# Transformer layers with routed experts: the order of queries and keys, scores and transposes of two pairs of heads, and the bank that the second pair's queries and keys are written to

## Chip, cores and metric

One core of one Trainium2 chip runs the whole kernel. The metric is the device time of one execution in microseconds. "us" below is microseconds. The core's engines are TensorE (PE in the rows; PEld is its weight load), VectorE (DVE), ScalarE (ACT), GpSimd (POOL) and SyncE (SP). Each engine takes its own instructions strictly in the order in which the program issues them, and waits on semaphores where another engine's result is needed; so a wait holds up everything issued behind it on that engine.

## What is computed

The input is 8 sequences of 256 tokens with 128 features. There are two stages, each an attention and then a feed-forward layer with 8 routed experts:

```python
x = x + attention_a(layernorm(x))   # 16 heads of 64, learned relative bias, softmax
x = x + experts(layernorm(x))       # one of 8 experts for each token, relu, gate
x = x + attention_b(layernorm(x))   # causal in blocks, keys and values from a 128-wide latent
x = x + experts(layernorm(x))
```

In the attention, for each head: `scores = q @ k.T * scale + bias` (or a causal mask), `softmax`, `@ v`, and then the output projection over all heads. All matrices are float32; the products with weights are made from three passes of high and low parts (`three`), and the high parts are made by ScalarE and the low ones by VectorE.

## The kernel before

The unit of the attention is a pair of heads of one sequence: a stage has NB = 8 sequences with 8 pairs each, NU = 64 units. Every engine runs a function `step(s)` for s = 0, 1, 2, ..., and in each step works on several units at once, so that the units overlap as in a pipeline. U0 and B0 are the number of units and sequences before the stage. The order within a step is written out by hand for each engine. Here an even step and the odd step behind it are called a round; e is the even unit and o the odd unit of a round.

For unit u the work goes like this:
- TensorE, `QK(u)`: queries and keys, six matmuls, into one bank of PSUM, `PT_` = ps[0]. Before it writes, it waits until the unit before has been copied out (`a_t`).
- ScalarE, `T(u)` (line 825): copies the bank to `a_qk[u % 2]`.
- TensorE, `S(u)` (line 528): the scores of the two heads, eight matmuls on 64 rows each, into a bank for each head: ps[1] and ps[2] for an even unit, ps[3] and ps[7] for an odd one. The two heads lie in the two halves of the array.
- VectorE, `S(u)` (line 1148): adds bias or mask, takes the row minimum of the negated scores and frees the banks (`v_mn`).
- ScalarE, `expo(u)` (line 857): exponentials and row sums, two steps later. VectorE, `weigh` (line 1159): reciprocals. GpSimd, `weigh` (line 315): normalises.
- TensorE, `TR(u)` (line 419), four steps later: eight transposes (six in the causal stage) into ps[4] and ps[5]; ScalarE copies the first head's (line 844), VectorE the second's (line 1177).
- TensorE, `PV(u)` (line 565): eight matmuls with weights of 64 columns. ScalarE and VectorE take the result apart in `keep` (lines 779 and 1028).

Around that, once for each sequence of 8 units: `values` (four times, 512 columns), the layer norm's transposes (`pre_b`), the latent (`pre_c`, stage 1 only), the output projection `out` (24 matmuls), its transposes back `out_2`, the second norm (`sums`, `post_a`, `post_b`), the router's logits (`post_c`), counts (`post_d`) and places (`choose`, `place` on VectorE, for some sequences).

TensorE's order in a round is, before the change: QK(e), values, pre_b, counts or logits, TR(e-4), out | QK(o), pre_c, out_2, post_b, TR(o-4), S(e), S(o), PV(e-4), PV(o-4). The bar divides the even from the odd step. VectorE's: keep, pre_b, post_a, TR(e-4), choose or place | pre_c, out_2, TR(o-4), reciprocals of e-2, `sums`, `pre_a2`, S(e), S(o), reciprocals of o-2, `pre_a`. VectorE's part of the logits (line 1215), `choose` and `place` are in `routes`, the last call of a step.

Small results of TensorE go to banks that `spare` hands out: `turn` is the list of banks of the step, in the order in which they are taken, and `claim` makes TensorE wait until the bank's last reader is done (`held`). The scores claim their banks in the same way.

Of the kernel before, what the change touches and what calls it, by code (L numbers as in the profile page):

```python
# [47 lines left out]
QUARTERS = (0, 2, 1, 3)  # L48
VALUES = [{2: [(0, 0)], 3: [(0, 2)], 4: [(0, 1), (0, 3)]}, {0: [(0, 0)], 1: [(0, 2)], 2: [(0, 1)], 4: [(0, 3)]}]
for _v in VALUES:  # L50
    _v |= {8 * b + 2 * i - 2: [(b, n)] for b in range(1, NB) for i, n in enumerate(QUARTERS)}
VALUE_NO = {(b, n): 4 * b + i for b in range(NB) for i, n in enumerate(QUARTERS)}
# [60 lines left out]
def build(nc, t):  # L113
# [291 lines left out]
    def spare(use, done, n, bank=None):  # L405

        if bank is None:
            bank = turn.pop(0)
            turn.append(bank)
        bank_of[use] = bank  # L410
        return claim(bank, done, n)
# [31 lines left out]
    def pe_steps(st):  # L443
# [29 lines left out]
        def values(b, n):  # L473
            k = 4 * B0 + VALUE_NO[(b, n)] + 1
            j, half_ = n // 2, n % 2
            if st == 0 and b == 0 and k <= 2:
                bank_of[("v", st, b, n)] = 3 + k
                PX = PP[k - 1]
            else:
                PX = spare(("v", st, b, n), a_vs, k)  # L480
            key_ready(b)
            if b == 0:
                pe.wait_ge(a_wv, 3 if st else 2)
                pe.wait_ge(v_wv, 3 if st else 2)
            r = slice(512 * half_, 512 * half_ + 512)
            c = slice(128 * j, 128 * j + 128)
            three(PX[:, :], kH[b % 2][:, c], kL[b % 2][:, c], wvh[:, r], wvl[:, r]).then_inc(t_v, 1)

        def QK(u):

            b, c = divmod(u, 8)
            if c == 0:
                pe.wait_ge(a_x, B0 + b + 1)
                pe.wait_ge(v_x, B0 + b + 1)
                key_ready(b)
            if st == 0 and u in (0, 4):
                pe.wait_ge(a_m, 2 + u // 2)
                pe.wait_ge(v_m, 2 + u // 2)
            if U0 + u:
                pe.wait_ge(a_t, U0 + u)  # L500
            r, r2_ = slice(128 * c, 128 * c + 128), slice(1024 + 128 * c, 1024 + 128 * c + 128)
            if U0 + u != NU:
                three(PT_[:, 0:256], wqkh[:, r], wqkl[:, r], a_xth[b % 2][:, :], a_xtl[b % 2][:, :])
            three(PT_[:, 256:512], wqkh[:, r2_], wqkl[:, r2_], kH[b % 2][:, :], kL[b % 2][:, :]).then_inc(t_t, 1)

# [196 lines left out]
        def step(s):  # L702
            n = s - F0
            turn[:] = (7, 3) if s < 0 or s >= NU else (3, 7, 1, 2) if s % 2 else (1, 2, 3, 7)
            if 0 <= s < NU:
                QK(s)
            if st == 0 and s == 0:
                value_weights()
# [4 lines left out]
            if st and (b := pre_at(s, "c", st)) is not None:  # L713
                pre_c(b)
                if b == 0:
                    first_queries()
            if (b := at(s, 13)) is not None and b < NB - 1:
                out_2(b)
            if s < NU:
# [68 lines left out]
    def act_steps(st):  # L788
# [10 lines left out]
        def pre_b(b):  # L799
            act.wait_ge(t_x, B0 + b + 1)  # L800
            inputs_free(b)
            if st and b >= 2:
                act.wait_ge(t_lat, b - 1)
            act_high(a_xth[b % 2][:, :], ps[bank_of[("x", B0 + b)]][:, 0:256], a_x)

        def pre_c(b):
            act.wait_ge(t_lat, b + 1)
            inputs_free(b)
            act_high(a_lth[b % 2][:, :], ps[bank_of[("l", b)]][:, 0:256], a_l)

# [10 lines left out]
        def T(u):  # L821
            act.wait_ge(t_t, U0 + u + 1)
            if U0 + u >= 2:
                act.wait_ge(t_s, U0 + u - 1)
            act.copy(a_qk[(U0 + u) % 2][:, :], PT_[:, :]).then_inc(a_t, 1)  # L825

        def values(b, n):
            j, half_ = n // 2, n % 2
            r = slice(512 * half_, 512 * half_ + 512)
            act.wait_ge(t_v, 4 * B0 + VALUE_NO[(b, n)] + 1)  # L830
            if B0 + b >= 2:
                act.wait_ge(t_pv, U0 + 8 * (b - 2) + 8)
            act.copy(a_v[b % 2][:, j, r], ps[bank_of[("v", st, b, n)]][:, :]).then_inc(a_vs, 1)

# [11 lines left out]

        def expo(u, heads=(0, 1)):
            U = U0 + u
            ring, mn, sm = a_ring[U % 4], a_mn[U % 4], a_sm[U % 4]
            for hh in heads:  # L850
                act.wait_ge(v_mn, 2 * (U0 + u) + hh + 1)
                if U >= 4 and hh == 0:
                    act.wait_ge(v_rs, U0 + u - 3)
                for it in range(2):
# [3 lines left out]
                                       bias=mn[:, q], scale=-1.0, accum_out=sm[:, q])  # L858
            if 1 in heads:
                i.then_inc(a_ex, 1)  # L860

        def out(b):
            act.wait_ge(t_out, 7 * st + b + 1)
            if 7 * st + b:
                act.wait_ge(t_o2, 7 * st + b)
            act.copy(a_oT[:, :], ps[bank_of[("o", B0 + b)]][:, 0:256]).then_inc(a_oTs, 1)

        def post_b(b):
            act.wait_ge(t_pp, B0 + b + 1)
            if B0 + b:  # L870
                act.wait_ge(t_lg, B0 + b)
            act.copy(a_pT[:, :], ps[bank_of[("p", B0 + b)]][:, 0:256]).then_inc(a_pTs, 1)

        def post_d(b):
# [3 lines left out]
            if r:  # L878
                act.wait_ge(v_used, r)
            act.copy(cnt[:, 0:2 * n8], ps[bank_of[("cnt", r)]][:, 0:2 * n8]).then_inc(a_cnt, 1)  # L880

        def extra(s):
            for g in range(2 if s == 4 else 0):
                act.wait_ge(t_wo, g + 1)
                act_high(wo[:, 4 * g:4 * g + 4, 0:128],
                         ps[bank_of[("wo", g)]][:, :].rearrange("p (c n) -> p c n", c=4), a_wo)

# [5 lines left out]
        def XT(g):  # L893
            n = 128 * (GROUPS[g][1] - GROUPS[g][0])
            act.wait_ge(t_fx, NG * st + g + 1)
            if NG * st + g >= 2:
                act.wait_ge(t_fh, NF * (st - (g < 2)) + GROUPS[g - 2][1])
            act.copy(f_xt[g % 2][:, 0:n], ps[bank_of[("xt", st, g)]][:, 0:n]).then_inc(a_fx, 1)

# [45 lines left out]
        def step(s):  # L945
# [19 lines left out]
            if not (s % 2 and 3 <= s < NU):  # L965
                if st and (b := pre_at(s, "c", st)) is not None:
                    pre_c(b)
                if s < NU:
                    after(s)
# [124 lines left out]
    def dve_steps(st):  # L1094
# [18 lines left out]
        def pre_b(b):  # L1113
            low(a_xtl[b % 2][:, :], ps[bank_of[("x", B0 + b)]][:, 0:256], a_xth[b % 2][:, :], a_x, B0 + b + 1, v_x)

        def pre_c(b):
            low(a_ltl[b % 2][:, :], ps[bank_of[("l", b)]][:, 0:256], a_lth[b % 2][:, :], a_l, b + 1, v_l)

# [72 lines left out]
        def out_2(b):  # L1191
            xx = x[:, 2 * b:2 * b + 2, :]
            dve.wait_ge(t_o2, 7 * st + b + 1)
            dve.tensor_tensor(xx, ps[bank_of[("o2", B0 + b)]][:, 0:256].rearrange("p (a d) -> p a d", a=2), xx,
                              ALU.add).then_inc(v_res, 1)
# [15 lines left out]
        def post_c(b):  # L1211
            dve.wait_ge(t_lg, B0 + b + 1)
            if st == 0 and b == 0:
                dve.wait_ge(d_ln, 48)
            dve.tensor_tensor(
                lg[:, 2 * b:2 * b + 2, :],
                ps[bank_of[("lg", B0 + b)]][:, 0:16].rearrange("p (t e) -> p t e", t=2),
                brb[:, :].rearrange("p (t e) -> p t e", t=1).broadcast_to((128, 2, NE)), ALU.add).then_inc(v_lg, 1)
# [122 lines left out]
        def step(s):  # L1341
# [203 lines left out]
```

## Time and profile before

| | us |
|---|---|
| median of 3 runs | 686.56 |
| lowest and highest | 685.88, 688.58 |
| the profiled execution, whole | 687.1 |
| its span on the core | 685.9 |
| TensorE busy in it | 652.9 |
| ScalarE busy in it | 533.3 |
| VectorE busy in it | 482.1 |
| GpSimd busy in it | 358.8 |

Stage 0's attention lies from about 13 to 295 us, its experts to about 370 us; stage 1's attention goes from there to about 615 us, its experts to the end. The starts of matmuls are recorded and their ends are modelled, so matmuls overlap in the record; where TensorE's own rate matters, the distance between starts is what to read.

### The profile page before, as it was taken

To read this page: it belongs to the slowest core of one execution; us is meant where nothing else is said; L and a number is where in the kernel's file an instruction comes from. 1 tells how busy PE (TensorE), PEld (TensorE's weight loads), DVE (VectorE), ACT (ScalarE), POOL (GpSimd) and SP (SyncE) were. 2 spreads that over 40 slices of the span, in tenths; PEclk is the share of its full clock that TensorE was granted. 3 is DMA by queue.
4 is the path that set the end of the run, shared out by engine and by line. 5 is a ranking of instruction groups with operands and counts; after the bars stand their busy time and mean duration, and the time that the engine had idled before them with its cause. 6 is when DMAs were issued, how large, how long until landed. Compare 5 with 4: busy or idle time off the path is not lost.

```text
span 685.9 us, 17753 instructions
## 1 busy us (share of the span) xinstructions
PE 652.9 (95%) x5406; PEld 549.8 (80%) x5406; DVE 482.1 (70%) x2145; ACT 533.3 (78%) x1774; POOL 358.8 (52%) x672
## 2 busy tenths in 40 slices
PE   6899999999999999989898999999999999989897
PEld 5678787888888888778796788878888888868886
DVE  4876767776786767877564676687868776896644
ACT  3888888787887978765573998898989898885464
POOL 3444545465556554635452555464755575553645
PEclk9999999999999999999998999999999999999999
DMA  9999999997000000134411000000000000031130
GB/s 266 303 304 304 231 284 308 300 293 216 1 2 17 17 1 5 37 87 161 126 43 55 2 2 1 1 3 9 17 11 1 10 24 3 17 87 44 58 106 13
DMA packets 67468, 64.65 MB, mean 94 GB/s; under 512 B 7793, under 2 KB 63998, under 8 KB 67120
## 3 DMA queue, kind: packets, MB, share of 16 engines
q1 hardware_dynamic: 62624, 56.41, 29.7%
q0 software_dynamic: 3136, 6.34, 2.7%
q10 hardware_dynamic: 1616, 0.79, 0.5%
q8 instruction: 45, 0.74, 0.5%
q14 instruction: 47, 0.39, 0.2%
HBM read 19.93 MB, written 44.75 MB: 94 GB/s over the span
## 4 chain that ended last, share of the span: by engine, by line
PE 82%; DVE 9%; issue 3%; ACT 2%; POOL 1%; DMA 1%; another core or an unknown queue 1%; SPq 0%; DVEq 0%; POOLq 0%; ACTq 0%
PE ps L419 16%; PE ps L565 14%; PE ps L528 14%; PE ps L414 10%; PE ps L416 8%; PE ps L415 8%; PE ps L668 5%; PE ps L682 4%; DVE ring L1148 2%; DMA wvn<-in_w_qkv 1%; PE ps L602 1%; PE ps L620 1%; ACT f_ht L906 1%; DVE f_ys L1314 1%
## 5 line engine op out<-in xcount | busy, mean ns | idle before, releaser
L315 POOL TENSOR_SCALAR ring<-ring,rs 128x256 f32<-128x256 f32 (+1 forms) x500 | 218.1, 453 | 221.2 <-DVE rs L1159 220.8
L857 ACT ACTIVATE ring<-ring,mn 128x256 f32<-128x256 f32 (+1 forms) x512 | 243.5, 489 | 0.0
L419 PE MATMUL ps<-ident,ring 128*128 128x128 f32 x896 | 120.4, 274 | 2.5 <-POOL ring L315 2.4
L528 PE MATMUL ps<-qk 64*128 64x256 f32 (+1 forms) x1024 | 115.0, 363 | 0.2 <-ACT qk L825 0.2
L565 PE MATMUL ps<-pt,v 128*64 128x256 f32 (+1 forms) x1024 | 111.9, 359 | 1.9 <-DVE pt L1175 1.3
L419 PEld LDWEIGHTS ps<-ident,ring 128*128 128x128 f32 x896 | 102.4, 142 | 8.2 <-POOL ring L315 3.5
L857 ACT ACTIVATION_READ_ACCUMULATOR ring<-ring,mn 128x1 f32 x512 | 104.5, 204 | 0.0
L565 PEld LDWEIGHTS ps<-pt,v 128*64 128x64 f32 x1024 | 65.8, 136 | 46.1 <-issue 14.5
L528 PEld LDWEIGHTS ps<-qk 64*128 64x128 f32 x1024 | 82.5, 187 | 18.0 <-issue 9.3
L825 ACT COPY qk<-ps 128x512 f32<-128x512 f32 x128 | 74.8, 585 | 24.9 <-PE ps L416 23.3
L1148 DVE CUSTOM_DVE_ANT_0 ring<-ps,cm 128x128 f32<-128x128 f32 (+1 forms) x256 | 73.5, 350 | 6.0 <-PE ps L528 6.0
L1177 DVE COPY pt<-ps 128x512 f32<-128x512 f32 x64 | 44.1, 689 | 35.1 <-PE ps L419 35.1
L906 ACT ACTIVATE f_ht<-ps,f_w 128x128 f32<-128x128 f32 x136 | 38.1, 373 | 35.2 <-PE ps L668 33.6
L414 PE MATMUL ps<-xth,wqkh 128*128 128x256 f32 x192 | 65.2, 340 | 0.0
L682 PE MATMUL ps<-w,f_ht 128*128 (+1 forms) x400 | 53.2, 278 | 4.1 <-ACT f_ht L906 2.4
L1148 DVE CUSTOM_DVE_ANT_0 ring<-ps,T 128x256 f32<-128x256 f32 x136 | 55.5, 417 | 0.0
L416 PE MATMUL ps<-xtl,wqkh 128*128 128x256 f32 x192 | 54.4, 283 | 0.0
L415 PE MATMUL ps<-xth,wqkl 128*128 128x256 f32 x192 | 54.1, 282 | 0.0
L779 ACT ACTIVATE oh<-ps 128x512 fp32r<-128x512 f32 x64 | 38.3, 599 | 20.0 <-PE ps L565 20.0
L682 PEld LDWEIGHTS ps<-w,f_ht 128*128 128x128 f32 x400 | 48.3, 192 | 6.2 <-issue 6.0
L414 PEld LDWEIGHTS ps<-xth,wqkh 128*128 128x128 f32 x192 | 36.4, 190 | 18.6 <-issue 17.4
L1148 DVE CUSTOM_DVE_ANT_1 ring<-ps,T 128x256 f32<-128x256 f32 x120 | 50.0, 417 | 0.0
(209 smaller groups left out, 1350.3 us busy)
## 6 DMA issues: line engine op xcount, KB each, us to landing
xs_scratch<-padt SPq DMA_DIRECT2D x16, 2064.0 KB, 21.6
f_xs<-xs_scratch SPq DMA_DIRECT2D x50, 129.0 KB, 2.4
w<-in_W SPq DMA_DIRECT2D x16, 256.0 KB, 6.2
xs_scratch<-padt SPq DMA_DIRECT2D x2, 1677.0 KB, 20.3
T<-in_bias SPq DMA_DIRECT2D x2, 512.0 KB, 8.2
T<-in_bias SPq DMA_DIRECT2D x1, 1024.0 KB, 10.8
bu<-in_w_kv_up SPq DMA_DIRECT2D x1, 1024.0 KB, 8.2
row<-in_x SPq DMA_DIRECT2D x1, 768.0 KB, 12.8
```

The costliest lines, as they stand in the source:

```text
L315: i = pool.tensor_scalar(ring[:, hh, it, 0:w], ring[:, hh, it, 0:w], rs[:, q], 1.0, ALU.mult, ALU.mult)
L414: pe.matmul(out, ah, bh, start=first, stop=False)
L415: pe.matmul(out, al, bh, start=False, stop=False)
L416: return pe.matmul(out, ah, bl, start=False, stop=last)
L419: return pe.transpose(out, src, ident[:, :])
L528: i = pe.matmul(PS[u % 2][hh][:, 256 * it:256 * it + w], qk[rows, 128 * it:128 * it + 128], qk[rows, 256:256 + w], start=True, stop=True)
L565: i = pe.matmul(PO[64 * hh:64 * hh + 64, col + lo:col + 256], a_v[b % 2][:, jt, 128 * c + 64 * hh:128 * c + 64 * hh + 64], a_pt[(U0 + u) % ...
L682: i = pe.matmul(y_bank(n)[:, 0:128], f_ht[n % 3][:, 128 * f:128 * f + 128], w2[:, bass.ds(e * 4 + f, 1), :].rearrange("p a n -> p (a n)"), ...
L825: act.copy(a_qk[(U0 + u) % 2][:, :], PT_[:, :]).then_inc(a_t, 1)
L857: i = act.activation(ring[:, hh, it, 0:w], ring[:, hh, it, 0:w], ACT.Exp, bias=mn[:, q], scale=-1.0, accum_out=sm[:, q])
L906: i = act.activation(f_ht[n % 3][:, r], h_bank(n)[:, r], ACT.Relu, bias=first_layer(n)[:, 640 + f:641 + f])
L1148: i = dve.tensor_tensor_reduce(ring[:, hh, it, 0:w], bank[:, 256 * it:256 * it + w], table(st, 2 * c + hh, it), 1.0, BIG, ALU.add, ALU.min ...
```

## The change

1. TensorE: `QK(e)` and `QK(o)` come together in the even step. `QK(o)` writes to ps[7], the bank of the second head's scores of the odd unit, and so waits until VectorE has read the scores of unit o-2 from it; `QK(e)` keeps ps[0]. ScalarE copies both together.
2. TensorE: `S(e)` comes first in the odd step, ahead of TR(o-4); `S(o)` comes behind TR(o-4) as before. VectorE takes S(e) first in the odd step too, and S(o) where both were.
3. The spare banks of a step: (3, 1, 2) in even steps, (0, 1) in odd ones, where they were (1, 2, 3, 7) and (3, 7, 1, 2).
4. `out_2` moves behind `S(o)` on TensorE, and behind TR(o-4) on VectorE.
5. Values that lay in odd steps move to even ones (one in either stage).
6. ScalarE: the exponentials of a unit are made in one go behind TR, where the even unit's second head came in the odd step; `post` and `pre` work lies at one place.

TensorE's order in a round after it: QK(e), QK(o), values, pre_b, counts or logits, TR(e-4), out | S(e), pre_c, post_b, TR(o-4), S(o), out_2, PV(e-4), PV(o-4).

```diff
+    PQ = (ps[0], ps[7])
...
         def QK(u):
 
+            claim(7 * (u % 2), a_t, U0 + u + 1)
             b, c = divmod(u, 8)
...
-            if U0 + u:
-                pe.wait_ge(a_t, U0 + u)
...
-                three(PT_[:, 0:256], wqkh[:, r], wqkl[:, r], a_xth[b % 2][:, :], a_xtl[b % 2][:, :])
+                three(PQ[u % 2][:, 0:256], wqkh[:, r], wqkl[:, r], a_xth[b % 2][:, :], a_xtl[b % 2][:, :])
...
-            turn[:] = (7, 3) if s < 0 or s >= NU else (3, 7, 1, 2) if s % 2 else (1, 2, 3, 7)
-            if 0 <= s < NU:
+            turn[:] = (7, 3) if s < 0 or s >= NU else (0, 1) if s % 2 else (3, 1, 2)
+            if s % 2 == 0 and 0 <= s < NU:
                 QK(s)
+                QK(s + 1)
+            if s % 2 and 1 <= s < NU:
+                S(s - 1)
...
-            if (b := at(s, 13)) is not None and b < NB - 1:
-                out_2(b)
             if s < NU:
                 after(s)
             if 4 <= s < NU + 4:
...
             if (b := at(s, 12)) is not None and b < NB - 1:
                 out(b)
             if s % 2 and 1 <= s < NU:
-                S(s - 1)
                 S(s)
+            if (b := at(s, 13)) is not None and b < NB - 1:
+                out_2(b)
...
# ScalarE
-            if 0 <= s < NU:
+            if s % 2 == 0 and 0 <= s < NU:
                 T(s)
+                T(s + 1)
...
-            if s % 2 and 3 <= s < NU:
-                if st and (b := pre_at(s, "c", st)) is not None:
-                    pre_c(b)
-                after(s)
-                expo(s - 3, (1,))
...
             if 2 <= s <= NU:
-                expo(s - 2, (0, 1) if s % 2 or s == NU else (0,))
+                expo(s - 2)
...
# VectorE
+            if s % 2 and 1 <= s < NU:
+                S(s - 1)
             if (b := pre_at(s, "b", st)) is not None:
                 pre_b(b)
...
-            if (b := at(s, 13)) is not None and b < NB - 1:
-                out_2(b)
...
             if 4 <= s < NU + 4:
                 TR(s - 4)
+            if (b := at(s, 13)) is not None and b < NB - 1:
+                out_2(b)
...
             if s % 2 and 1 <= s < NU:
-                S(s - 1)
                 S(s)
```

## Rows read from the trace of the kernel before

**Rows 1.** The page, busy time, and its 40 slices for TensorE and its clock.

```profile
PE 652.9 (95%) x5406; PEld 549.8 (80%) x5406; DVE 482.1 (70%) x2145; ACT 533.3 (78%) x1774; POOL 358.8 (52%) x672
...
PE   6899999999999999989898999999999999989897
...
PEclk9999999999999999999998999999999999999999
```

**Rows 2.** Busy time by stretches, columns named in the first line.

```profile
core 0: us, PE busy (x) PEld busy (x) DVE busy (x) ACT busy (x) POOL busy (x), PEclk, DMA share, GB/s
...
100.00:150.00 50.00, 50.00 (x406) 40.45 (x405) 38.69 (x173) 42.13 (x132) 28.56 (x54) 1.00 1.10 304
...
450.00:500.00 50.00, 49.86 (x445) 41.40 (x445) 38.16 (x198) 45.57 (x169) 31.08 (x65) 1.00 0.04 12
```

**Rows 3.** TensorE's waits, whole span: total us, times, longest.

```profile
PE ps L414 <- DVE mn L1148: 2.8, 2, 2.3
...
PE ps L528 <- ACT qk L825: 0.2, 1, 0.2
```

**Rows 4.** Timeline, TensorE, one round of stage 0: start, us, line, work, count.

```profile
124.75 0.28 PE L416 MATMUL ps<-xtl,wqkh 128*128 128x256 f32 x1
124.87 1.03 PE L419 MATMUL ps<-ident,ring 128*128 128x128 f32 x8
125.83 2.00 PE L528 MATMUL ps<-qk 64*128 64x256 f32 x16
127.76 1.95 PE L565 MATMUL ps<-pt,v 128*64 128x256 f32 x16
129.64 0.39 PE L414 MATMUL ps<-xth,wqkh 128*128 128x256 f32 x1
129.86 0.27 PE L415 MATMUL ps<-xth,wqkl 128*128 128x256 f32 x1
129.97 0.28 PE L416 MATMUL ps<-xtl,wqkh 128*128 128x256 f32 x1
```

**Rows 5.** Timeline, TensorE, the same round, short windows that cut groups apart.

```profile
125.63 0.27 PE L419 MATMUL ps<-ident,ring 128*128 128x128 f32 x1
...
126.15 0.38 PE L528 MATMUL ps<-qk 64*128 64x256 f32 x2
...
127.45 0.38 PE L528 MATMUL ps<-qk 64*128 64x256 f32 x2
...
128.03 0.39 PE L565 MATMUL ps<-pt,v 128*64 128x256 f32 x2
...
129.32 0.39 PE L565 MATMUL ps<-pt,v 128*64 128x256 f32 x2
```

**Rows 6.** Timeline, a round with logits: the even unit's transposes and VectorE behind.

```profile
150.83 1.07 PE L419 MATMUL ps<-ident,ring 128*128 128x128 f32 x8
...
151.94 0.69 DVE L1177 COPY pt<-ps 128x512 f32<-128x512 f32 x1 [1.54 <-PE ps L419]
...
152.55 0.17 DVE L1215 TENSOR_TENSOR lg<-ps,brb 128x16 f32<-128x16 f32 x1
```

**Rows 7.** Timeline, a round with `out` and `sums`, stage 0.

```profile
135.01 0.29 PE L416 MATMUL ps<-ol,wo 128*128 128x256 f32 x1
...
135.33 0.37 ACT L866 COPY oT<-ps 128x256 f32<-128x256 f32 x1 [1.64 <-PE ps L416]
...
136.30 0.42 DVE L1194 TENSOR_TENSOR row<-ps,row 128x256 f32<-128x256 f32 x1 [3.01 <-PE ps L419]
...
137.87 0.26 DVE L1033 BATCH_NORM_STATS2 s<-row 128x6 f32<-128x128 f32 x1
...
138.99 0.41 DVE L1148 CUSTOM_DVE_ANT_1 ring<-ps,T 128x256 f32<-128x256 f32 x1
```

**Rows 8.** Timeline, VectorE, a round with `place`.

```profile
124.96 0.16 DVE L1066 COPY bas<-run 128x8 f32<-128x8 f32 x1
...
126.95 0.17 DVE L1081 CAST posi<-posf 128x4 int32<-128x4 f32 x1
127.03 0.69 DVE L1177 COPY pt<-ps 128x512 f32<-128x512 f32 x1
```

**Rows 9.** Timeline, a round of stage 1.

```profile
445.67 1.60 PE L528 MATMUL ps<-qk 64*128 64x128 f32 x16
...
447.20 1.52 PE L565 MATMUL ps<-pt,v 128*64 128x256 f32 x16
...
447.73 0.28 DVE L1148 CUSTOM_DVE_ANT_0 ring<-ps,cm 128x128 f32<-128x128 f32 x1
...
448.65 0.39 PE L414 MATMUL ps<-xth,wqkh 128*128 128x256 f32 x1
```

More of the change, by code:

```diff
@@ L48 @@
 QUARTERS = (0, 2, 1, 3)
-VALUES = [{2: [(0, 0)], 3: [(0, 2)], 4: [(0, 1), (0, 3)]}, {0: [(0, 0)], 1: [(0, 2)], 2: [(0, 1)], 4: [(0, 3)]}]
+VALUES = [{2: [(0, 0)], 3: [(0, 2)], 4: [(0, 1)], 6: [(0, 3)]}, {0: [(0, 0)], 2: [(0, 2)], 4: [(0, 1), (0, 3)]}]
 for _v in VALUES:
-    _v |= {8 * b + 2 * i - 2: [(b, n)] for b in range(1, NB) for i, n in enumerate(QUARTERS)}
+    for _s, _q in ((8 * b + 2 * i - 2, (b, n)) for b in range(1, NB) for i, n in enumerate(QUARTERS)):
+        _v.setdefault(_s, []).append(_q)
 VALUE_NO = {(b, n): 4 * b + i for b in range(NB) for i, n in enumerate(QUARTERS)}
@@ L409, in spare @@
             turn.append(bank)
-        bank_of[use] = bank
+        bank_of[use] = ps[bank]
         return claim(bank, done, n)
@@ L476, in values @@
             if st == 0 and b == 0 and k <= 2:
-                bank_of[("v", st, b, n)] = 3 + k
-                PX = PP[k - 1]
+                PX = bank_of[("v", st, b, n)] = PP[k - 1]
             else:
@@ L498, in QK @@
                 pe.wait_ge(v_m, 2 + u // 2)
-            if U0 + u:
-                pe.wait_ge(a_t, U0 + u)
             r, r2_ = slice(128 * c, 128 * c + 128), slice(1024 + 128 * c, 1024 + 128 * c + 128)
             if U0 + u != NU:
-                three(PT_[:, 0:256], wqkh[:, r], wqkl[:, r], a_xth[b % 2][:, :], a_xtl[b % 2][:, :])
-            three(PT_[:, 256:512], wqkh[:, r2_], wqkl[:, r2_], kH[b % 2][:, :], kL[b % 2][:, :]).then_inc(t_t, 1)
+                three(PQ[u % 2][:, 0:256], wqkh[:, r], wqkl[:, r], a_xth[b % 2][:, :], a_xtl[b % 2][:, :])
+            three(PQ[u % 2][:, 256:512], wqkh[:, r2_], wqkl[:, r2_], kH[b % 2][:, :], kL[b % 2][:, :]).then_inc(t_t, 1)
         def first_queries():
@@ L803, in pre_b @@
                 act.wait_ge(t_lat, b - 1)
-            act_high(a_xth[b % 2][:, :], ps[bank_of[("x", B0 + b)]][:, 0:256], a_x)
+            act_high(a_xth[b % 2][:, :], bank_of[("x", B0 + b)][:, 0:256], a_x)
         def pre_c(b):
@@ L808, in pre_c @@
             inputs_free(b)
-            act_high(a_lth[b % 2][:, :], ps[bank_of[("l", b)]][:, 0:256], a_l)
+            act_high(a_lth[b % 2][:, :], bank_of[("l", b)][:, 0:256], a_l)
         def keep(u):
@@ L824, in T @@
                 act.wait_ge(t_s, U0 + u - 1)
-            act.copy(a_qk[(U0 + u) % 2][:, :], PT_[:, :]).then_inc(a_t, 1)
+            act.copy(a_qk[(U0 + u) % 2][:, :], PQ[u % 2][:, :]).then_inc(a_t, 1)
         def values(b, n):
@@ L832, in values @@
                 act.wait_ge(t_pv, U0 + 8 * (b - 2) + 8)
-            act.copy(a_v[b % 2][:, j, r], ps[bank_of[("v", st, b, n)]][:, :]).then_inc(a_vs, 1)
+            act.copy(a_v[b % 2][:, j, r], bank_of[("v", st, b, n)][:, :]).then_inc(a_vs, 1)
         def TR(u):
@@ L845, in TR, with expo @@
             i.then_inc(a_pt0, 1)
-        def expo(u, heads=(0, 1)):
+        def expo(u):
             U = U0 + u
             ring, mn, sm = a_ring[U % 4], a_mn[U % 4], a_sm[U % 4]
-            for hh in heads:
+            for hh in range(2):
                 act.wait_ge(v_mn, 2 * (U0 + u) + hh + 1)
@@ L858, in expo @@
                                        bias=mn[:, q], scale=-1.0, accum_out=sm[:, q])
-            if 1 in heads:
-                i.then_inc(a_ex, 1)
+            i.then_inc(a_ex, 1)
         def out(b):
@@ L865, in out @@
                 act.wait_ge(t_o2, 7 * st + b)
-            act.copy(a_oT[:, :], ps[bank_of[("o", B0 + b)]][:, 0:256]).then_inc(a_oTs, 1)
+            act.copy(a_oT[:, :], bank_of[("o", B0 + b)][:, 0:256]).then_inc(a_oTs, 1)
         def post_b(b):
@@ L871, in post_b @@
                 act.wait_ge(t_lg, B0 + b)
-            act.copy(a_pT[:, :], ps[bank_of[("p", B0 + b)]][:, 0:256]).then_inc(a_pTs, 1)
+            act.copy(a_pT[:, :], bank_of[("p", B0 + b)][:, 0:256]).then_inc(a_pTs, 1)
         def post_d(b):
@@ L879, in post_d @@
                 act.wait_ge(v_used, r)
-            act.copy(cnt[:, 0:2 * n8], ps[bank_of[("cnt", r)]][:, 0:2 * n8]).then_inc(a_cnt, 1)
+            act.copy(cnt[:, 0:2 * n8], bank_of[("cnt", r)][:, 0:2 * n8]).then_inc(a_cnt, 1)
         def extra(s):
@@ L885, in extra @@
                 act_high(wo[:, 4 * g:4 * g + 4, 0:128],
-                         ps[bank_of[("wo", g)]][:, :].rearrange("p (c n) -> p c n", c=4), a_wo)
+                         bank_of[("wo", g)][:, :].rearrange("p (c n) -> p c n", c=4), a_wo)
         def products(*ns):
@@ L897, in XT @@
                 act.wait_ge(t_fh, NF * (st - (g < 2)) + GROUPS[g - 2][1])
-            act.copy(f_xt[g % 2][:, 0:n], ps[bank_of[("xt", st, g)]][:, 0:n]).then_inc(a_fx, 1)
+            act.copy(f_xt[g % 2][:, 0:n], bank_of[("xt", st, g)][:, 0:n]).then_inc(a_fx, 1)
         def relu(n):
@@ L964, in step @@
                 pre_b(b)
[L965 to L969, printed above, removed]
+            if st and (b := pre_at(s, "c", st)) is not None:
+                pre_c(b)
+            if s < NU:
+                after(s)
             if 4 <= s < NU + 4:
@@ L1113, in pre_b @@
         def pre_b(b):
-            low(a_xtl[b % 2][:, :], ps[bank_of[("x", B0 + b)]][:, 0:256], a_xth[b % 2][:, :], a_x, B0 + b + 1, v_x)
+            low(a_xtl[b % 2][:, :], bank_of[("x", B0 + b)][:, 0:256], a_xth[b % 2][:, :], a_x, B0 + b + 1, v_x)
         def pre_c(b):
-            low(a_ltl[b % 2][:, :], ps[bank_of[("l", b)]][:, 0:256], a_lth[b % 2][:, :], a_l, b + 1, v_l)
+            low(a_ltl[b % 2][:, :], bank_of[("l", b)][:, 0:256], a_lth[b % 2][:, :], a_l, b + 1, v_l)
         def keep(u):
@@ L1193, in out_2 @@
             dve.wait_ge(t_o2, 7 * st + b + 1)
-            dve.tensor_tensor(xx, ps[bank_of[("o2", B0 + b)]][:, 0:256].rearrange("p (a d) -> p a d", a=2), xx,
+            dve.tensor_tensor(xx, bank_of[("o2", B0 + b)][:, 0:256].rearrange("p (a d) -> p a d", a=2), xx,
                               ALU.add).then_inc(v_res, 1)
@@ L1216, in post_c @@
                 lg[:, 2 * b:2 * b + 2, :],
-                ps[bank_of[("lg", B0 + b)]][:, 0:16].rearrange("p (t e) -> p t e", t=2),
+                bank_of[("lg", B0 + b)][:, 0:16].rearrange("p (t e) -> p t e", t=2),
                 brb[:, :].rearrange("p (t e) -> p t e", t=1).broadcast_to((128, 2, NE)), ALU.add).then_inc(v_lg, 1)
@@ L1224, in extra @@
             for g in range(2 if s == 4 else 0):
-                low(wo[:, 4 * g:4 * g + 4, 128:256], ps[bank_of[("wo", g)]][:, :].rearrange("p (c n) -> p c n", c=4),
+                low(wo[:, 4 * g:4 * g + 4, 128:256], bank_of[("wo", g)][:, :].rearrange("p (c n) -> p c n", c=4),
                     wo[:, 4 * g:4 * g + 4, 0:128], a_wo, g + 1, v_wo)
```

## Prediction

> **What bounds the kernel now.** First the page's busy times and slices: TensorE is busy 652.9 of 685.9 us, and its clock was granted in full nearly everywhere [rows 1]. Then the stretches, since a mean over the span says nothing of a stage: in the attention of stage 0 TensorE is busy 50.00 of 50 us, in that of stage 1 49.86; ScalarE has 42.13 and 45.57 there, VectorE 38.69 and 38.16 [rows 2]. Then its waits: for the copy of queries and keys, which a second bank is to hide, it waited 0.2 us in the whole span, and for a bank of scores 2.8 us, of which 2.3 at once at the start [rows 3]. So in both attentions the time is what TensorE needs to issue its matmuls one behind the other, and no other engine holds it up. What the change can win by waits is about 3 us; what it adds to TensorE's own order counts in full.
>
> That order has a price that busy time hides, since the ends of matmuls are modelled. It is in the distances of starts [rows 4, 5]. A transpose follows a QK matmul after 0.12 us (124.75 to 124.87), which is a QK matmul's own distance (129.86 to 129.97): going between these two costs nothing. Eight transposes would take 0.87 us at 0.11 each (124.87 to 125.63 is seven), but the scores start 0.20 behind the last transpose (125.63 to 125.83), 0.09 too late. The second couple of score matmuls comes 0.32 behind the first (125.83 to 126.15), where the block has 0.21 as a rule (16 matmuls, 8 couples, from 125.83 to 127.45 are 1.62 for seven, one of them the long one): 0.10 more. So entering the scores' half arrays from whole ones costs 0.20 us. From scores to PV it is 0.31 instead of 0.21 and then 0.27 instead of 0.21 (127.45, 127.76, 128.03): 0.15. From PV back to QK it is 0.32 (129.32 to 129.64) and then 0.22 instead of 0.12 (129.64 to 129.86): 0.20. Other rounds show the same distances to 0.02 us: it is a fixed cost of the switch and no wait.
>
> The Trainium skill says the same in "TensorEngine Tiling (Array Packing)", Key Properties: changing the tiling mode drains TensorE. The trace agrees with 0.15 to 0.20 us for each switch. By that rule alone the change would cost its added switches, and by the trace the number is the first two terms below.
>
> **The change part by part.** *The switches.* Before, a round has QK, TR, QK, TR, then S S, then PV PV: whole, scores, PV, whole. After it has QK QK TR, then S, then TR, then S, then PV PV: one way out of the scores and one into them more. Into: 0.20 us as above. Out of the scores into transposes does not occur before. Its bounds: 0.10 (the drain alone, the second transpose hidden) and 0.20 (as PV to QK). I take 0.15, since a transpose's load is shorter than that of a QK matmul. Together 0.35 us (0.30 to 0.40). It counts in rounds whose odd step has a TR, 30 in either stage: 60 x 0.35 = 21.0 us. Nothing hides it, as TensorE is the bound.
>
> *out_2 behind S(o).* Two transposes between scores and PV, where they lay among whole matmuls: out of scores 0.15, into PV 0.15, less the switch scores to PV that was there, 0.15: 14 x 0.15 = 2.1 us (7 sequences in either stage).
>
> *The spare banks, and S(e) close behind them.* Even steps take banks 3, 1, 2, in that order; S(e) claims 1 and 2 first thing in the odd step, where before it came two long blocks later. What was put into 1 or 2 just ahead must be read first.
> (a) Logits: values take 3, logits take 1. VectorE reads them in `routes`, behind its copy of the even unit's transposes. The last of those transposes starts at 150.83 + 0.76 = 151.59; the copy runs from 151.94, the logits' reader from 152.55 to 152.72 [rows 6]. S(e) would start at 151.79 and now can at about 152.8: 1.0 us, for six sequences in either stage whose logits have scores behind them, 12 x 1.0 = 12.0 us. It could be less only if VectorE took the copy earlier, and that one waits for TensorE.
> (b) `out`: values 3, pre_b 1, out 2 (for the last one out takes 1; the same). S(e) is right behind, and bank 2 is free when ScalarE has copied oT. The last matmul starts at 135.01, the copy runs 135.33 to 135.70 [rows 7]; S(e) would start at 135.21 and now at 135.78: 0.57 us, 14 x 0.57 = 8.0 us.
>
> *The second bank for QK.* QK(o) now waits until VectorE has read S(o-2)'s second head; before, that reader had a whole round. In a plain round VectorE reads S(o) within 1.4 us (four of 0.345) and TensorE needs 1.85 (PV) and 0.9 (QK(e)) until then: free. Not so where `sums` stands ahead of S(o) on VectorE. Count from the end of S(e) on TensorE: TR 1.02, S(o) 1.04, out_2 0.37, so out_2 is done and seen at 2.65; VectorE adds it (0.4), takes reciprocals (0.1) and the norm chain, 137.87 to 138.99 = 1.12 [rows 7], then S(o) 1.4: done at 5.7. TensorE has PV from 2.43 to 4.3 and QK(e) to 5.2, and would start QK(o) there: 0.5 us late. In stage 1 scores and PV are shorter (1.53 and 1.45 us a round instead of 1.93 and 1.88) [rows 4, 9]: 0.7. 14 x 0.6 = 8.4 us.
>
> *S(e) ahead of the copy on VectorE.* `place` takes 124.96 to 127.03, 2.1 us [rows 8], at the end of an even step. Before, the copy for PV came first in the odd step and the scores behind it, with a whole PV block to spare. After: from the last transpose of the even step, copy done at 1.0, place 3.1, S(e) 4.5, copy 5.15; TensorE wants it for PV(o) at 0.2 + 1.0 + 1.0 + 1.0 + 0.95 = 4.2, so 0.95 late, and S(o) with the norm behind it comes late for the next QK(o) too, in part: 1.2 us, three times in either stage, 7.2 us.
>
> *Edits at nothing.* ScalarE's two copies together, its exponentials in one go, and the values moved keep their counts. ScalarE is idle for 9% of stage 1's stretch [rows 2] and TensorE's rounds of 7 us grow by 5% from the switches alone, so its work stays covered; if not, see the rivals. The start (waits of 2.8 us before) may go either way by 2 us: 0. The end of a stage and the experts are untouched.
>
> *The sum:* 21.0 + 2.1 + 12.0 + 8.0 + 8.4 + 7.2 = 58.7 us. The profiled execution took 687.1, so 745.8; it stands 0.5 above the median of the runs, so 745.3. I say 745.
>
> **The rivals.** *Only the switches count* (17 in 100). The waits of S(e) and QK(o) fall where another lateness already was, or VectorE and ScalarE run ahead: 687 + 23 = 710 us. For it: each wait is under 1.1 us, and four are computed from single rounds. Against it: TensorE has no slack in the rows in which they could vanish.
> *Only the waits count* (8 in 100). Weights for the transposes are loaded in the shadow of the scores: 687 + 36 = 722 us. Against it: all four kinds of switch in the trace cost.
> *ScalarE becomes the bound of stage 1* (6 in 100). It is at 45.57 of 50 us [rows 2], and its copies now stand directly ahead of TensorE's next block: the transposes of o need e's copy, which comes behind two QK copies and the values' one. If each of 28 rounds loses 0.6 more: 745 + 17 = 762 us and above.
> *No change* (3 in 100): the new order's costs are hidden somehow: 687 us.
> *Faster* (4 in 100). The second bank lets TensorE go on while ScalarE copies. All it can win is the 0.2 us of the copy and the 2.8 us of the bank [rows 3]: 684 us. It decides only if the switch prices above are no prices of the switch. The rule it goes by is in the Trainium skill, "Perfetto Trace Analysis", Optimizing Tensor Performance: independent matmul groups should rotate through different banks, so that one's evacuation overlaps the next. The trace shows that the transposes between the two QK already do that here.
> The side opposite to my forecast is this last one.
>
> **How the numbers follow.** My forecast, switches and waits both, has 62 in 100, and a range of its own of 725 to 760: the switches between 0.30 and 0.40 us (3 us either way), the waits between a half and 1.3 times what I have. The range for 8 in 10 reaches down to the switches alone and up to the forecast with some of ScalarE: 708 to 762. What a measurement of this kernel can tell from no change is about 0.5%, 3.4 us. Slower than that: 62 + 17 + 8 + 6 = 93 in 100; within: 3; faster: 4.
>
> **What would show it.** In the changed trace: score blocks of eight matmuls, each with 0.20 ahead and 0.32 for its second couple; transposes 0.31 behind the last scores; TensorE waiting for DVE lg (12 times, 1.0 us), for ACT oT (14, about 0.5), for DVE mn ahead of QK (about 14) and for DVE pt ahead of PV (about 6). Busy shares of ScalarE and VectorE fall with the longer span, their busy times stay. The prediction is wrong if the scores start no later behind transposes, if these waits aren't there, or if the time is below 705 us.

## The result and the profile after

| | before | changed |
|---|---|---|
| median of the runs, us | 686.43 | 751.63 |
| lowest and highest, us | 685.88, 688.58 | 748.66, 753.22 |
| span of the profiled execution, us | 685.9 | 747.4 |
| TensorE busy, us | 652.9 | 680.5 |
| ScalarE busy, us | 533.3 | 543.1 |
| VectorE busy, us | 482.1 | 484.3 |

The changed kernel takes 1.0938 times as long, with a 95% interval of 1.0894 to 1.0983: 65 us slower. The profiled execution is the quickest of its four (748.7 us).

Busy times and slices of TensorE, the page of the changed kernel; they answer [rows 1]:

```profile
PE 680.5 (91%) x5406; PEld 546.6 (73%) x5406; DVE 484.3 (65%) x2145; ACT 543.1 (73%) x1774; POOL 358.5 (48%) x672
...
PE   4999999999999999979897899999999899889987
...
PEclk9999999999999999999999999999999999999999
```

The instructions are as many as before, and the clock was granted in full nearly everywhere in both executions, so no engine was given more to do or a slower clock. (ScalarE's busy time grew by 9.8 us, though its exponentials, the largest group, took no longer: 241.0 us, 243.5 before.) The stretches, in the columns of [rows 2], show that TensorE is no longer full and yet stays the engine that is busiest:

```profile
100.00:150.00 50.00, 46.86 (x360) 36.67 (x357) 30.55 (x134) 36.65 (x111) 22.00 (x44) 1.00 1.10 296
...
450.00:500.00 50.00, 47.06 (x395) 36.66 (x393) 33.34 (x171) 41.59 (x148) 24.95 (x55) 1.00 0.01 2
```

In 50 us TensorE now issues 360 matmuls where it issued 406, and is idle for 3 us of them. Over the whole span its busy time grew by 27.6 us and its idle time by 33.9 (from 33.0 to 66.9): the record calls a little less than half of the loss busy. The scores' first and last start in either stage, by their line (count; least, median and greatest ns; first and last start), say in which stage it lies, first before, then changed:

```profile
L528 PE MATMUL ps<-qk x512: 376/376/481, 13.3 to 289.2; 64*128 64x256 f32 x171
L528 PE MATMUL ps<-qk x512: 269/375/378, 372.8 to 609.3; 64*128 64x128 f32 x86, 64*128 64x256 f32 x85
```

```profile
L528 PE MATMUL ps<-qk x512: 376/376/792, 12.4 to 319.6; 64*128 64x256 f32 x171
L528 PE MATMUL ps<-qk x512: 272/375/378, 402.8 to 669.5; 64*128 64x128 f32 x86, 64*128 64x256 f32 x85
```

Stage 0's attention went from 275.9 to 307.2 us and stage 1's from 236.5 to 266.7: 31.3 + 30.2 = 61.5 of the 61.5 us by which the span grew. What lies between and behind them (83.6 and 76.6 us before, 83.2 and 77.9 after) is as long as it was.

TensorE's waits in the changed kernel (us in total, times, longest), which answer [rows 3]:

```profile
PE ps L528 <- issue: 11.5, 14, 0.9
PE ps L416 <- DVE mn L1144: 11.3, 18, 3.3
PE ps L528 <- ACT oT L867: 6.6, 12, 0.6
PE ps L565 <- DVE pt L1171: 5.9, 4, 2.2
...
PE ps L565 <- DVE pt L1173: 4.7, 6, 1.8
```

L528 is the scores, L416 the first matmul of QK, L565 PV; L1144 and L1173 are VectorE's scores and copy, lines 1148 and 1177 before; L1171 is the same copy in the causal stage. For these lines it was under 5 us before and is 40 now. The first has no releaser in the record; by their places 12 of the 14 are the wait for the logits' bank, and the other two belong to `out`, whose wait the third line shows 12 times. A round with logits shows it (start, us; in brackets the idle time before), and answers [rows 6]:

```profile
85.67 1.07 PE L421 MATMUL ps<-ident,ring 128*128 128x128 f32 x8
...
86.77 0.69 DVE L1173 COPY pt<-ps 128x512 f32<-128x512 f32 x1 [2.27 <-PE ps L421]
...
87.38 0.16 DVE L1211 TENSOR_TENSOR lg<-ps,brb 128x16 f32<-128x16 f32 x1
...
87.64 1.14 PE L528 MATMUL ps<-qk 64*128 64x256 f32 x8 [0.91 <-issue]
88.71 1.09 PE L421 MATMUL ps<-ident,ring 128*128 128x128 f32 x8
...
89.73 1.13 PE L528 MATMUL ps<-qk 64*128 64x256 f32 x8
```

S(e) starts 0.10 us after VectorE is done with the logits (87.38 + 0.16), and 1.18 after the last transpose (86.46) where it was 0.20. The same rows show the switches: from the first scores to the next ones it is 2.09 us, of which the sixteen matmuls at their own distances (0.84 and 0.87 us) account for 1.71. So a round pays 0.38 us here that two blocks of scores side by side do not. (Finer: two score matmuls start 0.216 us behind the two before them, not 0.21, and a round without a wait, with S(e) at 135.41 and S(o) at 137.49, then pays 0.34.)

### The profile page after: what moved, and what is told of

Its sections match the earlier page's. It is cut to its first block, busy times and chain, and to the rows that moved or that the text cites. A ratio compares the mean times of both kernels' runs of the same rounds, so it can differ in the third digit from the quotient of the medians.

```text
span 747.4 us, 17750 instructions
## 1 busy us (share of the span) xinstructions
PE 680.5 (91%) x5406; PEld 546.6 (73%) x5406; DVE 484.3 (65%) x2145; ACT 543.1 (73%) x1774; POOL 358.5 (48%) x672
## 4 chain that ended last, share of the span: by engine, by line
PE 75%; DVE 13%; issue 7%; ACT 3%; POOL 1%; DMA 1%; SPq 0%; another core or an unknown queue 0%; DVEq 0%; POOLq 0%; ACTq 0%
PE ps L421 15%; PE ps L528 14%; PE ps L565 10%; PE ps L416 10%; PE ps L418 7%; PE ps L417 7%; PE ps L668 5%; PE ps L682 4%; DVE ring L1144 4%; PE ps L620 1%; ACT f_ht L907 1%; PE ps L602 1%; DMA wkn<-in_w_qkv 1%; DVE mn L1144 1%; DVE pt L1173 1%
## 5 line engine op out<-in xcount | busy, mean ns | idle before, releaser
L859 ACT ACTIVATE ring<-ring,mn 128x256 f32<-128x256 f32 (+1 forms) x512 | 241.0, 482 | 0.0
L528 PE MATMUL ps<-qk 64*128 64x256 f32 (+1 forms) x1024 | 132.3, 377 | 18.9 <-issue 11.5
L421 PE MATMUL ps<-ident,ring 128*128 128x128 f32 x896 | 122.7, 277 | 1.7 <-POOL ring L317 1.7
L565 PE MATMUL ps<-pt,v 128*64 128x256 f32 (+1 forms) x1024 | 113.7, 360 | 11.0 <-DVE pt L1171 5.9
L528 PEld LDWEIGHTS ps<-qk 64*128 64x128 f32 x1024 | 79.7, 187 | 44.5 <-issue 40.4
L565 PEld LDWEIGHTS ps<-pt,v 128*64 128x64 f32 x1024 | 65.9, 136 | 54.7 <-issue 28.9
L859 ACT ACTIVATION_READ_ACCUMULATOR ring<-ring,mn 128x1 f32 x512 | 101.7, 199 | 0.0
L1144 DVE CUSTOM_DVE_ANT_0 ring<-ps,cm 128x128 f32<-128x128 f32 (+1 forms) x256 | 75.5, 350 | 31.8 <-PE ps L528 31.8
L416 PE MATMUL ps<-xth,wqkh 128*128 128x256 f32 x192 | 63.4, 330 | 11.3 <-DVE mn L1144 11.3
L1173 DVE COPY pt<-ps 128x512 f32<-128x512 f32 x64 | 44.0, 687 | 42.9 <-PE ps L421 42.9
L1144 DVE CUSTOM_DVE_ANT_1 ring<-ps,T 128x256 f32<-128x256 f32 x120 | 50.2, 418 | 31.9 <-PE ps L528 30.9
L416 PEld LDWEIGHTS ps<-xth,wqkh 128*128 128x128 f32 x192 | 36.2, 189 | 33.0 <-issue 17.4
L1144 DVE CUSTOM_DVE_ANT_0 ring<-ps,T 128x256 f32<-128x256 f32 x136 | 55.7, 419 | 0.0
L1024 DVE TENSOR_TENSOR ol<-ps,oh 128x512 fp32r<-128x512 f32 x64 | 43.4, 679 | 17.1 <-ACT oh L781 17.0
```

The source lines that it names most:

```text
L416: pe.matmul(out, ah, bh, start=first, stop=False)
L421: return pe.transpose(out, src, ident[:, :])
L528: i = pe.matmul(PS[u % 2][hh][:, 256 * it:256 * it + w], qk[rows, 128 * it:128 * it + 128], qk[rows, 256:256 + w], start=True, stop=True)
L565: i = pe.matmul(PO[64 * hh:64 * hh + 64, col + lo:col + 256], a_v[b % 2][:, jt, 128 * c + 64 * hh:128 * c + 64 * hh + 64], a_pt[(U0 + u) % ...
L859: i = act.activation(ring[:, hh, it, 0:w], ring[:, hh, it, 0:w], ACT.Exp, bias=mn[:, q], scale=-1.0, accum_out=sm[:, q])
L1144: i = dve.tensor_tensor_reduce(ring[:, hh, it, 0:w], bank[:, 256 * it:256 * it + w], table(st, 2 * c + hh, it), 1.0, BIG, ALU.add, ALU.min ...
```

## The experiments

All ratios are to the kernel before, run beside each kernel on its chip. The kernel before took 684.18 us beside experiments one to four and 686.73 beside the others, so kernels of the two groups are compared by their ratios.

**One: the pair of QK without the split scores.** From the changed kernel, S(e) goes back to S(o), behind TR(o-4), on TensorE and VectorE; `out_2` is given bank 0.

```diff
# TensorE and VectorE, in step(s)
-            if s % 2 and 1 <= s < NU:
-                S(s - 1)
...
             if s % 2 and 1 <= s < NU:
+                S(s - 1)
                 S(s)
...
-            PX = spare(("o2", B0 + b), v_res, NB * st + b + 1)
+            PX = spare(("o2", B0 + b), v_res, NB * st + b + 1, 0)
```

> The changed kernel with the scores of both units together again behind TR(o-4), on TensorE and VectorE; QK(e) and QK(o) stay together, the second bank stays, and out_2 takes bank 0. Theory 1 (the interleaving of scores and transposes costs: its switches, and the waits of S(e) that comes too early): the 21 us of switches, the 11 of the logits' bank, the 9 of out's bank and the 6 of place go; what stays is out_2's switch (2 us) and QK(o) waiting for VectorE, about 0.1 to 0.7 us in a few rounds: 692 to 702 us. Rival (the shared bank 7 costs: VectorE reads both units' scores late, so QK(o) waits 0.7 us in every one of 60 rounds): 725 to 740 us.

Measured: 751.49 us, ratio 1.098 (1.094 to 1.102). Neither theory's time, and the first one's is far off: without the interleaving the kernel is as slow as with it. TensorE's waits:

```profile
PE ps L416 <- DVE mn L1143: 35.0, 24, 2.9
PE ps L421 <- ACT pt L843: 9.2, 22, 0.6
PE ps L421 <- ACT pt L845: 6.2, 20, 0.4
```

The last two are new, and they say what S(e) does between the transposes. A round of it:

```profile
57.46 0.59 ACT L845 COPY pt<-ps 128x512 f32<-128x512 f32 x1
...
58.20 1.06 PE L421 MATMUL ps<-ident,ring 128*128 128x128 f32 x8 [0.38 <-ACT pt L845]
```

TR(o-4) writes the banks of TR(e-4), so it waits for ScalarE's copy. Before the change QK(o) stood between the two and covered that copy; the change takes QK(o) away, and S(e) has to stand in for it. By the starts the transposes are 0.54 us late here, more than the 0.38 us of idle time, since the idle time is counted only from the modelled end of the matmul before. The first wait is longest at the starts of the stages; otherwise it is 1.67 to 1.69 us in the rounds of stage 0 with `out_2` and 1.45 to 1.50 in those of stage 1, 14 in all, and under 1 us in a few others. So experiment six moves `out_2` back.

**Two: the split scores without the pair.** From the kernel before, on TensorE alone.

```diff
+            if s % 2 and 1 <= s < NU:
+                S(s - 1)
             if 4 <= s < NU + 4:
                 TR(s - 4)
...
             if s % 2 and 1 <= s < NU:
-                S(s - 1)
                 S(s)
```

> The kernel before with one move on TensorE alone: S(e) ahead of TR(o-4). QK(o) stays where it was with its bank, and so do the spare banks and the other engines. Theory 1 (each switch between whole and half arrays costs, 0.35 us a round for the two more): 686.5 + 60 x 0.35 = 707.5 us, and up to 3 us for logits whose bank is read late: 706 to 712 us; the trace has 0.31 from scores to transposes, 0.17 for the second transpose, 0.20 and 0.32 at the next scores. Rival (the loss of the change is waits alone, a switch is hidden): 686 to 690 us.

Measured: 711.43 us, ratio 1.039 (1.037 to 1.042), 27 us over the 684.2 of its own chip. The logits wait 2.4 us and another wait, for VectorE ahead of the second norm's transposes, 3.0:

```profile
PE ps L419 <- DVE ph L1045: 3.0, 8, 0.7
...
PE ps L528 <- DVE lg L1216: 2.4, 12, 0.2
```

The rest is the switches: in the scores' spans the growth is 11.8 us in stage 0 and 12.5 in stage 1, less these waits some 19 us, 0.32 a round. The medians of its own chip, 27.3 us less the same waits, give 22 us, 0.36 a round. The rival, in which switches are hidden, is out. The same distances stand in it as in the round above:

```profile
102.33 1.13 PE L528 MATMUL ps<-qk 64*128 64x256 f32 x8
103.39 1.09 PE L419 MATMUL ps<-ident,ring 128*128 128x128 f32 x8
104.41 0.92 PE L528 MATMUL ps<-qk 64*128 64x256 f32 x6
```

**Three: other spare banks in the changed kernel.**

```diff
-            turn[:] = (7, 3) if s < 0 or s >= NU else (0, 1) if s % 2 else (3, 1, 2)
+            turn[:] = (7, 3) if s < 0 or s >= NU else (0, 1) if s % 2 else (1, 2, 3)
...
-            PX = spare(("o", B0 + b), a_oTs, 7 * st + b + 1)
+            PX = spare(("o", B0 + b), a_oTs, 7 * st + b + 1, 3)
...
-            PX = spare(("lg", B0 + b), v_lg, B0 + b + 1)
+            PX = spare(("lg", B0 + b), v_lg, B0 + b + 1, 3 if b < NB - 2 else None)
```

> The changed kernel with other spare banks in even steps: (1, 2, 3) in place of (3, 1, 2), and bank 3 for the logits and for out, so that S(e) never claims what was written just ahead of it. Theory 1: the waits of S(e) go, 12 x 0.95 for the logits and 14 x 0.63 for out, 20 us: 751.6 - 20 = 731 us. Rival (these waits only take the place of later ones, since VectorE and ScalarE are behind anyway): 745 to 752 us, with the waits turning up at PV or QK.

Measured: 732.79 us, ratio 1.071 (1.067 to 1.074); near the first theory's time. Part of the 19 us below the changed kernel is the quicker chip: by the ratios it is 16 us, by the spans of the profiled executions 15.4. The waits for oT are gone and those ahead of the scores fell from 11.5 to 2.1, 16 us together; three waits of 0.45 us ahead of PV in stage 1 are new:

```profile
PE ps L416 <- DVE mn L1144: 10.2, 18, 2.2
PE ps L565 <- DVE pt L1171: 7.3, 7, 2.2
...
PE ps L565 <- DVE pt L1173: 4.2, 4, 1.8
...
PE ps L528 <- issue: 2.1, 3, 0.7
```

**Four: as three, and place, index and sums behind S(o) on VectorE.**

```diff
# VectorE, in step(s)
-            if (b := at(s, 13)) is not None and b < NB - 1:
-                sums(b)
...
             if s % 2 and 1 <= s < NU:
                 S(s)
+            if (b := at(s, 13)) is not None and b < NB - 1:
+                sums(b)
             if s % 2 and 3 <= s < NU:
                 weigh(s - 2)
+            if s % 2 and s < NU:
+                places(s - 1)
...
# in routes(s); places(s) holds place and index
+            if s >= NU:
+                places(s)
```

> As the one before, and on VectorE place, index (of steps below 64) and sums come behind S(o) in the odd step. Theory 1: the waits of PV for VectorE's copy (6 x 1.1 and 4 us with index) and of QK(o) behind sums (14 x 0.39 = 5.3) go too, about 16 us: 731 - 16 = 715 us, which is the kernel before plus its switches (23 us) and a slower start. Rival (VectorE is simply short of time in these rounds and the wait moves behind): 725 to 731 us.

Measured: 732.39 us, ratio 1.070 (1.067 to 1.074). No gain on experiment three, 1 us above the rival's range, yet not by its cause:

```profile
PE ps L421 <- DMA f_xs<-xs_scratch: 15.8, 4, 6.1
PE ps L416 <- DVE mn L1144: 6.7, 4, 3.2
...
PE ps L421 <- DVE ph L1040: 4.1, 2, 2.2
```

The waits for VectorE ahead of QK did go (18 became 4), and those of PV fell from 11.5 to 1.4 us. But a new one stands at the start of either stage's experts, 6.1 and 5.5 us: the rows that `index` computes are what the first gather needs. Another of 2 us, for `ph` of the last second norm, stands at the end of either attention.

**Five: as four, with index where the changed kernel has it; and the changed kernel again beside it.**

```diff
         def routes(s):
...
             if s >= NU:
                 places(s)
+            if s in INDEX:
+                index(INDEX[s])
 
         def places(s):
             if (b := post_at(s, "place")) is not None and b in ROUTED:
                 place(*ROUTED[b], NR * st + ROUTE_NO[b])
-            if s in INDEX:
-                index(INDEX[s])
```

> The changed kernel once more, beside the kernel before on the same chip as the next ones, so that they can be compared: ratio 1.094, 747 to 752 us.

Measured: 751.83 us, ratio 1.093 (1.088 to 1.097), the same as the first time.

> The kernel with the other spare banks, and on VectorE only place and sums behind S(o); index stays where the changed kernel has it, since with it moved the experts' first rows came 6 us late in either stage (the wait for f_xs). Theory 1: the 6 waits of PV (6.5 us) and the 14 of QK(o) (5.3 us) go, index's 4 us stay: 732.8 - 12 = 721 us, ratio 1.052 to 1.056. Rival (VectorE is short of time, the waits move): 728 to 733 us.

Measured: 724.4 us, ratio 1.054 (1.050 to 1.057), in the range of the first theory by the ratio; its time lies 3 us above, on a chip that is 2.5 us slower. The lines for VectorE's scores and copies:

```profile
PE ps L416 <- DVE mn L1144: 6.5, 4, 3.0
...
PE ps L565 <- DVE pt L1171: 3.7, 4, 2.3
PE ps L416 <- DVE ol L1024: 2.6, 5, 0.7
...
PE ps L565 <- DVE pt L1173: 2.0, 1, 2.0
```

The four waits ahead of QK that stay are all within the first rounds of a stage; two of the waits for the copy (2.0 and 2.3 us) are those of `index`; the wait for `ol` is new, before `out` in the step behind `place`, so a part of that wait has only moved.

**Six: the pair of QK alone once more, with out_2 where the kernel before has it.** As one, and `out_2` ahead of TR(o-4) on both engines.

> The kernel with QK(e) and QK(o) together and the scores together again, now with out_2 where the kernel before has it, ahead of TR(o-4) on both engines. In the first run of this kind TensorE waited 35 us for VectorE's scores ahead of QK(o) and 15 us for ScalarE's copies between TR(e-4) and TR(o-4). Theory A (out_2 behind the scores made VectorE start them late, in the 14 rounds of out_2): QK(o) waits 1.2 us less in these, out_2 waits 0.6 for oT: some 10 us less than before, 738 to 744 us; the waits between the transposes stay at 0.4 to 0.6 us a round, since QK(o) no longer covers ScalarE's copy. Theory B (VectorE's scores are late in every round, wherever out_2 is): 748 to 752 us.

Measured: 743.7 us, ratio 1.081 (1.077 to 1.084): theory A.

```profile
PE ps L416 <- DVE mn L1143: 13.3, 12, 2.9
PE ps L421 <- ACT pt L843: 9.2, 22, 0.6
PE ps L421 <- ACT pt L845: 6.8, 23, 0.4
...
PE ps L421 <- DVE ltl L1023: 5.6, 6, 0.9
PE ps L421 <- ACT oT L866: 4.4, 8, 0.6
```

QK's wait fell by 22 us, as `out_2` no longer holds VectorE's scores back; the wait for the copies is unchanged, and by the starts (about 0.5 us each, 45 of them) it is the largest part of the loss that is left, some 23 us. The time fell by only 12 us by the ratios, since `out_2` has waits of its own now: 4.4 us for oT and 5.6 us for `ltl`, the latent in bank 0, which this experiment also gives to `out_2`. The pair without the split scores still costs 8%, about 1 of it by that choice of bank.

**Seven: the second bank alone.** From the kernel before: QK(o) writes to ps[7], every step stays where it is, and the spare banks are (3, 1, 2) in odd steps and (1, 2, 3) in even ones.

> The kernel before with the second bank alone: QK(o) writes to ps[7], nothing moves, and the spare banks leave 7 out. Theory 1 (the bank's wait was 0.2 us in all, so the bank by itself is worth nothing, and VectorE has read bank 7 long before QK(o)): within 1 us of the kernel before, ratio 0.998 to 1.003. Rival (the bank costs or wins by itself): more than 3 us either way.

Measured: 687.82 us, ratio 1.0019 (1.0001 to 1.0038). Nothing worth speaking of either way: by itself the bank is no cause of the loss, which comes with the new order and, for 16 us of it, the spare banks chosen for it. The run isn't quite the bank alone. Without ps[7] among the spare banks, `out_2` falls to bank 1 in six rounds of stage 1, and S(e) starts 0.62 us late behind it, 3.7 us in all (3.3 us idle); without these the bank would gain 0.4% at most. Under the new order it does matter: QK(o)'s waits there (11.3 us) are for this bank.

## Why the prediction was right

Forecast 745 us, measured 751.6: within the range. The profiled execution, against which the sum was made, took 748.7 us where the sum gives 745.8: 61.6 us more than before, of a forecast 58.7. By the medians the rise is 65.2 us, 6.5 more than the sum; 3.6 of that lies between the executions: the profiled one of before took 0.7 us more than its median, that of the changed kernel 3.0 less. By its own terms, in us, the measured ones read in the changed kernel's trace as the distance between two starts of matmuls less their distance where nothing is waited for:

| term | forecast | measured |
|---|---|---|
| logits' bank ahead of S(e) | 12 x 1.0 = 12.0 | 6 x 0.98 + 6 x 0.91 = 11.3 |
| out's bank ahead of S(e) | 14 x 0.57 = 8.0 | 14 x 0.63 = 8.7 |
| QK(o) behind sums | 7 x 0.5 + 7 x 0.7 = 8.4 | 7 x 0.47 + 7 x 0.52 = 6.9 |
| VectorE's copy behind place and S(e) | 7.2 | 3 x 0.98 + 3 x 1.30 = 6.8 |
| switches, 60 rounds | 60 x 0.35 = 21.0 | about 21 by the distances, 19 to 22 by experiment two |
| out_2's switches | 2.1 | about 2 |
| start of the stages | 0 | 4 to 5 |
| VectorE's copy behind index, end of the stages | 0 | 2.6, of which the span grew 0.9 |

*The switches.* Scores to transposes, which the trace of before did not have, is 0.31 us, and the second transpose comes 0.17 behind the first: 0.10 + 0.06 as the prediction took between its bounds. Experiment two has this cost nearly by itself, with 5 us of waits, which settles the rival in which it is hidden. The drain that the Trainium skill names in "TensorEngine Tiling (Array Packing)", Key Properties, agrees with the 0.10 us of later start. That the other 0.06 us is a weight load no longer hidden, as the prediction took it, no run shows by itself. The prediction also counts four kinds of switch in the trace of before; it has the prices of three.

*The logits and out.* Both waits were foreseen at their place and to a tenth, and experiment three takes them away by naming other banks: about 16 us of the 65, for no other change.

*sums.* Right in stage 0, a third too large in stage 1 (0.7 against 0.52). A round of stage 0: out_2's transposes start at 151.81, and QK(o) 0.59 behind QK(e)'s last matmul instead of 0.12.

```profile
150.74 1.13 PE L528 MATMUL ps<-qk 64*128 64x256 f32 x8
151.81 0.44 PE L421 MATMUL ps<-ident,oT 128*128 128x128 f32 x2
152.17 1.95 PE L565 MATMUL ps<-pt,v 128*64 128x256 f32 x16
...
154.75 0.28 PE L418 MATMUL ps<-xtl,wqkh 128*128 128x256 f32 x1
155.34 0.39 PE L416 MATMUL ps<-xth,wqkh 128*128 128x256 f32 x1 [0.31 <-DVE mn L1144]
```

The same distance in stage 1 is 0.64, a wait of 0.52 where 0.7 was forecast. The prediction took off there what TensorE saves in scores and PV, but not what VectorE saves: its scores of a unit take 1.19 us (452.88 to 454.07) where the round above takes 1.46 (153.83 to 155.29), and from its adding of `out_2` to these scores it is 1.42 us instead of 1.55.

*place.* As forecast, and a row shows it: PV(o) waits 0.80 us idle for the copy that VectorE began at 139.61, behind place (to 138.28) and S(e):

```profile
138.11 0.17 DVE L1077 CAST posi<-posf 128x4 int32<-128x4 f32 x1
138.23 0.42 DVE L1144 CUSTOM_DVE_ANT_1 ring<-ps,T 128x256 f32<-128x256 f32 x1
...
139.61 0.69 DVE L1173 COPY pt<-ps 128x512 f32<-128x512 f32 x1
...
140.44 0.87 PE L565 MATMUL ps<-pt,v 128*64 128x256 f32 x6 [0.80 <-DVE pt L1173]
```

*What was set to nothing and was not.* The prediction put the start at nothing, "may go either way by 2 us". QK(o) now has the start's wait that values had (3.3 us at once, against 2.3) and a second of 0.7 us, and stage 1's first rounds wait for bank 7 too (0.9 and 1.8 us). It held the end of a stage untouched: it is not. `index` stands at the end of steps 60 and 62 as `place` does, so the copy that PV needs comes 1.9 and 2.2 us late (the row below), where the kernel before waited 0.7 and 0.8 at about that place. Experiment four shows that it can't simply be moved. The start is more than the whole shortfall of 2.9 us; `sums` was oversized by half of that. So the closeness of the total is in part luck: terms too large and terms left out cancel. The busy times that were to stay did so for VectorE (482.1 and 484.3 us), not for ScalarE (533.3 and 543.1).

```profile
322.75 1.08 PE L565 MATMUL ps<-pt,v 128*64 128x256 f32 x8 [1.75 <-DVE pt L1173]
```

*The rivals.* Only the switches, and only the waits, are both out: with most of the waits taken away 5.4% stay (five), and the waits of S(e) alone are worth 16 us (three), while the switches alone, in experiment two, cost the 19 to 22 us. ScalarE is not the bound: it has 41.59 of 50 us in stage 1, and no copy of it holds the transposes up in the changed kernel. Faster is out, and experiment seven shows what it would have rested on: the bank alone is worth nothing measurable. The transposes already stood between the two QK, and [rows 3] has 0.2 us of waiting for the copy; a second bank had nothing left to hide.

*What the prediction did not see* is what the two halves of the change owe each other. It treated the split of the scores as a cost alone and did not ask what it buys. (Its rival of ScalarE as the bound names the dependency, that the transposes of o need e's copy, but not that S(e) now covers it.) Experiments one and six show what: with QK(o) gone from between the two transposes, something has to stand there, or TensorE is idle for up to 0.6 us waiting for ScalarE's copy, and VectorE is late with both scores at once. The pair costs 8% without the split; the split costs 4% without the pair; together 9%, and 5.4% with banks and VectorE's order mended. None of them is faster than the kernel before. Where the last 5.4% goes is not taken apart fully: the switches are some 3 points of it, the starts and ends of the stages and the moved waits the rest.

## What to carry to other kernels

Where TensorE never waits, an order is worth what its matmuls' starts say, not what its busy time says: count the changes between whole and half arrays in a round before splitting a block to hide a wait, and keep the blocks of one kind together. A block moved nearer to a small producer (logits, a projection's end) inherits the bank that the producer's reader still holds; list for each claim who wrote the bank last and behind what its reader stands on its engine. And a block that seems to be merely in between may be the cover for someone's copy: ask that before moving it.

## What the runs showed of the hardware

Leaving half arrays for whole ones costs less where the whole-array work is transposes than where it is products with weights: the second transpose came 0.17 us behind the first instead of 0.11, the second QK matmul 0.22 instead of 0.12. The changed kernel has both behind scores, so that it isn't the kind of half array that is left: in stage 1 `pre_c` follows S(e), and its first product starts about 0.31 us behind the last scores, as a transpose does, the second 0.22 behind the first.

```profile
417.05 0.39 PE L416 MATMUL ps<-xth,kdh 128*128 128x256 f32 x1
417.27 0.27 PE L417 MATMUL ps<-xth,kdl 128*128 128x256 f32 x1
```

A switch's price isn't shown as idle time of the engine: in experiment two TensorE's busy time is 20.6 us greater than before (673.5 against 652.9) and its idle time 3.8, with 5 us of new waits in its attention. And a wait costs more than the idle time that the record gives it: S(e) behind the logits started 0.98 us late with 0.91 idle, QK(o) behind `sums` 0.47 late with 0.31 idle.
